# Query projection moved one step ahead of its consumers, from step 4 on, in a fused attention and feed-forward kernel

## The reference, cut to what matters

```
x = layernorm(x)
q = (x @ Wq.T).reshape(b, n, 16, 128)          # 16 heads of 128
kp, vp = split(x @ Wkv.T)                       # one key and one value for all heads
kh, vh = split(cumsum((x @ Wkvh.T) * decay))    # one factor per token and head
k = rope(kp * kh);  v = vp * vh;  q = rope(q)
p = softmax(causal(q @ k.T / sqrt(128)))
out = (p @ v) @ Wout.T
```

## Time and profile before

| what | us |
|---|---|
| three runs | 1096.25, 1095.37, 1092.69 |
| median | 1095.37 |
| the profiled execution's own time | 1093.13 |
| its span, first to last instruction | 1091.3 |
| TensorE busy | 1052.3 |
| GpSimd busy | 928.1 |
| VectorE busy | 872.8 |
| ScalarE busy | 861.5 |

### The profile page before, as it was taken

How to read it: one execution, slowest core, us unless ns; L and a number is a source line. 1 busy time by engine, 2 the same in 40 slices (tenths; PEclk the granted TensorE clock), 3 DMA queues, 4 the chain that set the end, 5 groups by cost and what they waited for, 6 DMA issues and landing times.

```text
span 1091.3 us, 25312 instructions
## 1 busy us (share of the span) xinstructions
PE 1052.3 (96%) x8010; PEld 1006.2 (92%) x8010; DVE 872.8 (80%) x2870; ACT 861.5 (79%) x2386; POOL 928.1 (85%) x846
## 2 busy tenths in 40 slices
PE   6899999999999999999999999999999899999997
PEld 6798999899989998998999999999999799999997
DVE  6879889989998998899889988987877656666654
ACT  4787888888888888887888788888878666666674
POOL 4698999899989999998999899999899658777685
PEclk9999999999999999999999999999999999999999
DMA  7450211021112110221021112111130000000001
GB/s 264 163 167 29 59 42 59 22 68 60 47 34 59 61 39 31 59 61 46 24 70 58 40 38 71 41 40 59 30 117 21 2 1 21 20 21 20 21 20 39
DMA packets 35124, 58.57 MB, mean 54 GB/s; under 512 B 3136, under 2 KB 16000, under 8 KB 34688
## 3 DMA queue, kind: packets, MB, share of 16 engines
q1 hardware_dynamic: 34992, 56.96, 16.6%
HBM read 50.92 MB, written 9.18 MB: 55 GB/s over the span
## 4 chain that ended last, share of the span: by engine, by line
POOL 59%; PE 21%; issue 17%; ACT 1%; DVE 1%; POOLq 0%; DMA 0%; ACTq 0%; DVEq 0%
POOL arena L575 15%; POOL arena L607 14%; POOL arena L596 14%; POOL arena L585 13%; PE psum L910 11%; PE psum L940 5%; PE psum L721 1%; PE psum L920 1%; PE psum L969 1%; POOL arena L545 1%; POOL X L566 1%; POOLq L297 0%; PE psum L747 0%; POOL arena L552 0%; PE psum L826 0%
## 5 line engine op out<-in xcount | busy, mean ns | idle before, releaser
L607 POOL TENSOR_TENSOR arena<-arena 128x768 f32<-128x768 f32 x128 | 196.5, 1535 | 18.8 <-DVE arena L1419 17.5
L575 POOL TENSOR_TENSOR arena<-arena,tables 128x512 f32<-128x512 f32 x128 | 165.7, 1295 | 39.4 <-ACT arena L1090 39.1
L585 POOL TENSOR_TENSOR arena<-arena 128x512 f32<-128x512 f32 x128 | 188.7, 1474 | 10.0
L1432 DVE SCALAR_TENSOR_TENSOR pt_split<-psum,vh_col,pt_split 128x256 fp32r<-128x256 f32 (+1 forms) x512 | 176.9, 407 | 0.0
L596 POOL TENSOR_TENSOR arena<-arena 128x512 f32<-128x512 f32 x128 | 165.2, 1290 | 2.6 <-DMA arena<-kh_rows 1.7
L826 PE MATMUL psum<-arena 128*128 128x256 f32 x512 | 154.6, 384 | 8.4 <-POOL arena L585 8.4
L1101 ACT ACTIVATE arena<-arena 128x256 f32<-128x256 f32 x256 | 128.6, 502 | 32.3 <-DVE arena L1409 25.5
L721 PE MATMUL psum<-wo_hi,o_hi 128*128 128x256 f32 x512 | 152.7, 298 | 0.0
L721 PE MATMUL psum<-xt_hi,wq_hi 128*128 128x256 f32 x512 | 146.0, 285 | 0.0
L721 PE MATMUL psum<-xt_lo,wq_hi 128*128 128x256 f32 x512 | 144.9, 283 | 0.0
L721 PE MATMUL psum<-xt_hi,wq_lo 128*128 128x256 f32 x512 | 144.9, 283 | 0.0
(11 more groups left out here) (170 smaller groups left out, 3508.1 us busy)
## 6 DMA issues: line engine op xcount, KB each, us to landing
arena<-kh_rows SPq DMA_DIRECT2D x127, 256.0 KB, 3.3
out<-spare SPq DMA_DIRECT2D x15, 256.0 KB, 2.1
arena<-w_rows SPq DMA_DIRECT2D x6, 512.0 KB, 4.7
X<-L_attn_Wout SPq DMA_DIRECT2D x1, 2048.0 KB, 14.5
X<-L_attn_x SPq DMA_DIRECT2D x1, 2048.0 KB, 13.0
arena<-L_attn_Wq SPq DMA_DIRECT2D x1, 1536.0 KB, 10.1
X<-L_attn_x SPq DMA_DIRECT2D x1, 1536.0 KB, 10.2
w_rows<-L_ffn_w_gate_up SPq DMA_DIRECT2D x3, 512.0 KB, 9.3
```

The lines of the kernel that those rows point to most:

```text
L575: nc.gpsimd.tensor_tensor(swap, swap, spread, ALU.mult).then_inc(q_sined, 1)
L585: nc.gpsimd.tensor_tensor(q_rot[p % 2], q_cos[p % 2], q_swap[p % 2], ALU.add).then_inc(q_roped, 1)
L607: nc.gpsimd.tensor_tensor(tb, tb, r.unsqueeze(3).to_broadcast([P, HP, 3, P]), ALU.mult).then_inc(p_ready, 1)
L1432: last = nc.vector.scalar_tensor_tensor(pt_lo[p % 2][:, o], b[:, i], vh[:, t, h:h + 1], pt_hi[p % 2][:, o].bitcast(F32), ALU.mult, ALU.sub ...
```

## The change

For steps 0 to 3 nothing changes. In step 4 two pairs are projected: pair 4 ahead of everything else of that step (before `turn` on TensorE, before `split_o` on VectorE and ScalarE), and pair 5 in the usual place. From then on the usual place of step n handles pair n+1, and step 127 projects nothing. `queries_cos` and `swap` go with the projection; `queries_sin`, `queries_add`, `score` and all later stages stay in their steps. The number and kind of instructions is the same. The waits keep their form with g one higher, so `queries_cos` of pair n+1, in step n, now waits for `queries_add` of pair n-1, which GpSimd does in that same step.

```diff
-LAG = dict(project=0, cos=0, swap=0, key=0, rope=1, score=1, softmax=2, turn=3, value=4, out=5)
+LAG = dict(key=0, rope=1, score=1, softmax=2, turn=3, value=4, out=5)
+JOIN = 4
...
+        def projected_at(g0, s, joining=False):
+
+            n = g0 + s
+            g = n if n < JOIN or joining else n + 1
+            if g < STEPS and (n == JOIN or not joining):
+                return g, g % PAIRS, g // PAIRS % 2
...
-            def project(g0, par, s):
+            def project(g0, s, joining=False):
 
-                at = pair_at(g0, s, LAG["project"])
+                at = projected_at(g0, s, joining)
                 if at:
-                    g, p, _ = at
+                    g, p, par = at
                     if p == 0:
-                        pe.wait_ge(xt_lo_done, g0 + PAIRS)
-                    if isinstance(g0, int) and g0 == 0:
+                        pe.wait_ge(xt_lo_done, g + PAIRS)
+                    if g < PAIRS:
                         pe.wait_ge(w_lo_done, 3 + p)
...
+                    project(g0, s, joining=True)
                     turn(g0, par, s)
                     value(g0, par, s)
...
-                    project(g0, par, s)
+                    project(g0, s)
                     score(g0, par, s)
...
+                    swap(g0, s, joining=True)
                     split_o(g0, s)
                     split_pt(g0, par, s)
                     swap(g0, s)
...
+                    queries_cos(g0, s, joining=True)
                     split_o(g0, s)
                     if not is_first(g0, s):
                         queries_cos(g0, s)
```

More of the change, by code:

```diff
@@ L1078, in copy_y, with swap @@
                 nc.scalar.activation(y_sb.rearrange("p t e -> p (t e)"), Y_BANK, ACT.Copy).then_inc(y_copied, PAIRS)
-            def swap(g0, s):
-                at = pair_at(g0, s, LAG["swap"])
+            def swap(g0, s, joining=False):
+                at = projected_at(g0, s, joining)
                 if at:
@@ L1385, in bias_y, with queries_cos @@
                     .then_inc(ln2_biased, PAIRS)
-            def queries_cos(g0, s):
-                at = pair_at(g0, s, LAG["cos"])
+            def queries_cos(g0, s, joining=False):
+                at = projected_at(g0, s, joining)
                 if at:
```

## The result

The changed kernel took 1099.72 us in the median of its runs (1096.54 to 1104.38), the kernel before 1094.73 us (1092.53 to 1096.97) on the same chips. The ratio is 1.0056, with a 95% interval of 1.0042 to 1.0070: slower by 5.0 us by the medians, where 3.8 us had been forecast (1099.2 us). The profiled execution took 1101.96 us, its span 1100.2 us at a mean granted clock of 0.989; before it was 1093.13, 1091.3 and 0.996.

What follows compares the result with a forecast made beforehand. TensorE, busy for 1052.3 of 1091.3 us, was taken to bound the kernel. Adding 3.0 us for the joining step and 0.8 for the port gave 1096.9 us profiled, 1099.2 us on the median; range 1090.0 to 1104.0.

Steps and rivals of the forecast that it cites:

- The steady part: Repeating steps: removing sin's wait for swap gains 0, since normalise then waits as much longer for invert_sums; lower end -6.8 us.
- The three idle stretches: TensorE's gaps in a 16-step cycle, a score 0.61 us, a turn 1.22, a score 0.20: all three stay.
- The first rival: GpSimd's freed time reaches TensorE and takes away 8.4 us of score waits: 1090.0 us, faster; chance 0.18.
- cos behind the add: Steady steps: queries_cos now needs the same step's add, which ends 0.54 us earlier in the tightest case; no new wait, cost 0.
- The joining step: Step 4, with two projections: the second cos starts 3.0 us later than the only one before; bounds 1.4 and 4.0 us.
- TensorE gets it through turn: Step 5: the joining delay reaches TensorE by the turn's wait for split_pt, at 50.4 instead of 47.39.
- The second rival: The joining step is hidden, by a bank emptied sooner or VectorE catching up: 1095.4 us, no change; chance 0.17.
- The end: Step 127 without projection saves TensorE 1.43 us, but it waits 1.4 us longer for GpSimd's add: value 0, lower end -1.4 us.
- The shared port: An earlier GpSimd add makes VectorE's comparison stand still, in six batches: 0 to 1.6 us, taken as 0.8.
- invert_sums and the gates operation behind it: VectorE operations queued behind the comparison, which stands still for up to 1.3 us; some 0.2 us may reach normalise of step 67.
- The third rival: The port turns against VectorE's small operations before the turn, 1.1 us in each of six chunks: 1105.8 us, slower; chance 0.13.
- four of the six stands: VectorE standstills for the port, 1.1 us per chunk in six chunks; four of them set the range's upper end, 1104.0 us.

Runs made afterwards that it cites:

- The two kernels with the scales moved: Three quantisation scales per weight chunk moved from VectorE to GpSimd: in the kernel before, 1084.75 us; in the changed kernel, 1090.31 us.
- with the clock held up: Changed kernel with 28 matmuls that nobody reads put into step 4 ahead of the second projection: 1099.00 us, ratio 1.0047.
- the release: Changed kernel with the one-step lead given back in step 120, which projects nothing, so the drain is that of the kernel before: 1097.82 us, ratio 1.0029.
- changed + scales: Changed kernel with the three quantisation scales per weight chunk moved from VectorE to GpSimd, between queries_add and normalise: 1090.31 us, ratio 0.9958.

## Why the prediction was right and where it was off

The median, 1099.72 us, lies 0.5 us above the forecast, but that nearness is in part luck. The terms did not each come out as set, and the forecast started from 1095.37, the median of three runs, where 16 runs gave 1094.73: the change itself cost 5.0 us and not 3.8.

- **The steady part, 0.** Right, and by its reason. normalise was forecast to wait 1.65 and 2.0 us in steps 59 and 60; it waits 1.69 and 2.09. The three idle stretches stayed. Measured: -0.4 us over 120 steps, the reason for which wasn't looked for. The first rival, that GpSimd's freed time reaches TensorE, is out: its sign was score waits gone from the steady part, and 4.5 of 4.7 us are there. The two kernels with the scales moved show it a second time.
- **cos behind the add.** Right: no wait of cos for it appeared, the least distance is 0.54 us as before, and steady steps kept their length.
- **The joining step, +3.0.** Right mechanism, right chain, 0.8 us too small. Forecast were a wait of 3 to 4 us before the second projection (3.84) and the second cos 3.0 us late (3.3; 3.2 with the clock held up). The step that failed is the one after it, "TensorE gets it through turn": TensorE ran at half the clock for part of the 4 us behind the wait and reached the turn of step 5 2.31 + 4.9 us late, busy and without a wait for split_pt; the forecast 50.4 became 52.3 on the same ruler, and 50.6 with the clock held up. Of the 4.9 us 3.8 were left at normalise of step 5, as the wait for L1357 took up the rest. The second rival, that the join is hidden, is out by the same rows.
- **The end, 0.** This is the term that failed, and in sign. "TensorE would wait 1.4 us longer instead" was right in length (0.45 to 1.85 us; the wait of 1.56 us that the prediction names is the score of step 128, which has no projection ahead of it in either kernel), but it was written as if the wait cost nothing else. In the profiled execution the drain cost 1.5 us by step 129 and 1.1 us more by the feed-forward, at clocks of 0.83, 0.74 and 0.57 where the kernel before had 1.00. By the ratios the release, which has no gap, took off 3.0 us, about 1 us of it in step 120 itself, and the twelve matmuls in the gap 2.3 us. It doesn't strike in each execution: three of the five profiles with the gap have no drop and no loss. This fits a spread of 7.8 us over the changed kernel's runs against 4.4 us before; its runs' mean granted clock goes from 0.994 (1096.5 us) to 0.984 (1104.4 us).
- **The shared port, +0.8.** Right as to who pays; 0 in place of 0.8 us. "invert_sums and the gates operation behind it" was the step that failed: the comparison was 0.70 us longer, not up to 1.3, the gates operation behind it took 0.23 us, since GpSimd was by then waiting (0.66 us in that step of before, and not the median's 1.42), and normalise gained by the add that was no longer stretched. I had counted the new payer's loss and left out the old payer's gain. The third rival, stands of VectorE's small operations at the turn, is out: the turn's wait is 1.22 us as before, and its waits from 150 to 800 us are 6.2 us in place of 6.4.

Sum by the profile: 3.8 for the join, -0.4 for the steady part, 0 for the port, 2.6 for the drain and 0.6 behind it, 6.6 us, beside 2.3 us of start-up chance. By the medians: 5.0 us; with the profile's 3.4 for join and steady part some 1.6 are left for the rest, and by their ratios the two experiments on the drain took off 2 to 2.3. The range's upper end was also set loosely: four of the six stands give 1103.6 us, not 1104.0. A forecast of 3.0 + 0.8 came near this because the port's 0.8 us stood where the drain's should have been.

What stays open: the release in step 120 brings its profile to 5.04 - 2.66 = 2.4 us in step 129, and the last block adds 1.0 us at the lower clock, which is near the 3.2 us by which its ratio stands above the kernel before; why the clock falls sooner at the end in three of the ten profiles (the changed kernel, the release, changed + scales) wasn't tested. What TensorE's clock is granted in the first 30 us wasn't controlled in any run. A join spread over several steps wasn't tried.

## What to carry to other kernels

A wait on an engine that doesn't set the pace is worth something only if no second wait stands behind it in the same step: read the next wait on that engine before counting the first. Taking a stage one step ahead cost its serial chain once, in each of the three steps tried, and left a step at the other end without that work; both holes stood on TensorE, and its clock could make them dearer than they were long. Here the useful move was another one: to look at what made TensorE wait (the turn, which waited for VectorE), and to put VectorE's small operations into the wait that GpSimd had anyway, for 11.0 us.

## What the runs showed of the hardware

- TensorE's granted clock fell behind an idle stretch of 3.8 us in mid-kernel (0.89 and then 0.69 by window), and in the drain behind one of 1.85 us, in two of five profiles (0.83 and 0.74 in the changed kernel's); behind one of 1.41 us in step 20 it stayed at 1.00. With matmuls that nobody reads in the gap it stayed at 1.00 in the three profiles that had them, and in the drain they paid for themselves (ratio 1.0035 against 1.0056, with intervals that overlap).
- In the last block it fell to 0.50 with TensorE at work (4.00 of 4.00 us busy from 1088 to 1092 us in the changed kernel), and a matmul took 0.41 us in place of 0.28.
- A TENSOR_SCALAR on 128x16 elements took 1.25 to 1.37 us on VectorE when GpSimd was at work, 0.16 us between two such, and 0.27 us on GpSimd. The long ones ended 0.03 us behind a GpSimd instruction.
- When GpSimd's add came 0.33 us ahead of VectorE's comparison instead of 0.34 us behind it, 0.86 us left the one (2.15 to 1.29) and 0.70 us came to the other (1.34 to 2.04).
- The first 30 us, in which all versions but one execute the same instructions, differ by up to 3.9 us between profiled executions, and the order is that of the granted clock from 20 to 28 us: -0.5 us at 1.00, 0 at 0.79, 2.3 to 3.0 at 0.57, 3.4 at 0.50.
